# Wide attention with its score channels laid as 128 plus a doubled 64, and transposes issued between the next tile's score matmuls

## The reference, cut to what matters

```python
def _L2_attn_ref(x, Wq, bq, Wk, bk, Wv, bv, Wc, bc):
    B, S, nd = x.shape
    q = jnp.einsum('bsd,ed->bse', x, Wq) + bq
    k = jnp.einsum('bsd,ed->bse', x, Wk) + bk
    v = jnp.einsum('bsd,ed->bse', x, Wv) + bv
    att = jnp.einsum('bqd,bkd->bqk', q, k) * nd ** (-0.5)
    att = jax.nn.softmax(att, axis=-1)
    y = jnp.einsum('bqk,bkd->bqd', att, v)
    y = jnp.transpose(y, (0, 2, 1)).reshape(B, S, nd)
    return jnp.einsum('bsd,ed->bse', y, Wc) + bc
t = t + _L2_attn_ref(_ln_t(t), ...)
```

## Time and profile before

| | us |
|---|---|
| median of 3 executions | 8461.63 |
| lowest, highest | 8458.88, 8468.84 |
| span of the profiled execution | 8460.6 |
| TensorE (PE) busy with matmuls, share of the span | 7417.9, 88% |
| the wide attention's part of the span (first constant issued to last output stored) | about 3369 to 4928 |

### The profile page before, as it was taken

One profiled execution on the slowest core, in us unless ns is written; L12 is line 12 of the kernel. 1 busy time (PEld: TensorE's weight loads), 2 busy tenths in 40 slices (PEclk: granted clock), 3 DMA queues, 4 the chain that ended last, 5 costly groups with the idle time before them and its releaser, 6 DMA issues. The chain is left out here.

```text
span 8460.6 us, 164061 instructions
## 1 busy us (share of the span) xinstructions
PE 7417.9 (88%) x53035; PEld 3625.5 (43%) x53035; DVE 4769.0 (56%) x7714; ACT 3185.4 (38%) x5336; POOL 2338.1 (28%) x2558
## 2 busy tenths in 40 slices
PE   6799999999996775799999970997799999999987
PEld 4233333333333552576666760775433333333326
DVE  6777777777772401232232243114677777777766
ACT  2166666666663241222222210212444444444432
POOL 0011111111111000000000003002388888888861
PEclk8699999999998786899999965998899999999986
DMA  4211111111114314000000031114611111111113
GB/s 118 58 33 33 33 33 33 33 33 33 33 29 95 104 46 132 27 13 13 26 1 17 1 119 54 52 49 135 200 31 30 30 31 29 30 30 31 30 50 105
DMA packets 414311, 426.01 MB, mean 50 GB/s; under 512 B 76199, under 2 KB 386635, under 8 KB 408590
## 3 DMA queue, kind: packets, MB, share of 16 engines
q1 hardware_dynamic: 331790, 339.52, 14.2%
q0 software_dynamic: 62400, 59.16, 2.8%
q10 hardware_dynamic: 19712, 21.53, 0.8%
HBM read 253.37 MB, written 166.55 MB: 50 GB/s over the span
## 5 line engine op out<-in xcount | busy, mean ns | idle before, releaser
L624 DVE TENSOR_REDUCE softmax_part_max<-softmax_ring 128x1 f32<-128x512 f32 (+1 forms) x2880 | 1727.2, 634 | 494.0 <-PE softmax_ring L534 464.0
L2421 DVE TENSOR_TENSOR retention_decayed<-retention_scores,retention_decay_table 128x768 f32<-128x768 f32 x1728 | 1655.4, 958 | 475.0 <-PE retention_scores L2381 475.0
L2440 POOL TENSOR_TENSOR retention_decayed<-retention_third,retention_decay_table 128x384 f32<-128x384 f32 x1728 | 1723.4, 997 | 456.7 <-ACT retention_third L2462 415.5
L664 ACT ACTIVATE softmax_probs<-softmax_scores 128x768 f32<-128x768 f32 x1728 | 1399.2, 811 | 885.8 <-PE softmax_scores L553 847.3
L2462 ACT COPY retention_third<-retention_scores 128x384 f32<-128x384 f32 x1728 | 827.9, 479 | 1276.6 <-PE retention_scores L2381 1276.6
L534 PE MATMUL softmax_ring<-softmax_k_next,softmax_q_next 96*128 96x512 bf16 (+1 forms) x2880 | 1086.5, 379 | 139.7 <-DVE softmax_part_max L624 49.7
L2394 PE MATMUL retention_sums<-retention_decayed,retention_v_piece 128*32 128x288 f32 x13824 | 1197.8, 418 | 0.5 <-POOL retention_decayed L2440 0.5
L2381 PE MATMUL retention_scores<-retention_q_half,retention_k_piece 96*128 96x384 bf16 x5184 | 1145.7, 330 | 29.4 <-DMA retention_v_piece<-ret_v 29.3
L565 PE MATMUL softmax_sums<-softmax_probs,softmax_v_piece 128*32 128x192 f32 x13824 | 930.2, 343 | 0.6 <-ACT softmax_result L653 0.5
L553 PE MATMUL softmax_scores<-softmax_q_third,softmax_k_piece 99*128 99x384 bf16 x3456 | 870.8, 333 | 5.9 <-ACT softmax_probs L664 5.9
L2381 PEld LDWEIGHTS retention_scores<-retention_q_half,retention_k_piece 96*128 96x128 bf16 x5184 | 366.6, 98 | 947.2 <-issue 832.2
(11 more groups left out here) (299 smaller groups left out, 6483.4 us busy)
## 6 DMA issues: line engine op xcount, KB each, us to landing
ret_v<-ret_proj_values SPq DMA_DIRECT2D x8, 1728.0 KB, 8.8
retention_v_piece<-ret_v SPq DMA_DIRECT2D x144, 96.0 KB
softmax_q_third<-rope_q SPq DMA_DIRECT2D x192, 54.0 KB
softmax_q_next<-rope_q POOLq DMA_DIRECT2D x64, 162.0 KB, 3.9
softmax_k_piece<-rope_k SPq DMA_DIRECT2D x192, 54.0 KB
softmax_k_next<-rope_k POOLq DMA_DIRECT2D x64, 162.0 KB, 5.5
ret_q<-ret_proj_parts SPq DMA_DIRECT2D x48, 216.0 KB
ret_k<-ret_proj_parts SPq DMA_DIRECT2D x48, 216.0 KB
```

Source lines behind the costliest of these rows:

```text
L624: nc.vector.reduce_max(part_max[:, j, c:c + 1], ring[m % 2][:, 0:CHUNKS[c][1]], axis=X)\
L664: nc.scalar.activation(probs[n % 4][:, :].rearrange("p (c q) -> p c q", c=2), scores[n % 2][:, :, 0:QC], ACT.Exp, scale=scale).then_inc(ex ...
L2421: nc.vector.tensor_tensor(weights[n % 4][:, 0:2 * QC].rearrange("p (c q) -> p c q", c=2), scores[n % 2][:, 0:2, 0:QC], table[:, table_at(n ...
L2440: nc.gpsimd.tensor_tensor(weights[n % 4][:, 2 * QC:HALF], third[n % 3][:, :], table[:, at:at + QC], ALU.mult)\
```

## The change

- The 192 channels of queries and keys are laid as 128 rows (part 0) plus 64 rows (part 1), and the 64 stand twice, on rows 0 to 63 and on rows 64 to 127. For this `wqk` is loaded in three pieces with the last 64 channels placed twice, the projections write 128 rows instead of 96, and `qk_t` has 128 rows.
- A tile's scores are now five matmuls over 128 channels (`long_part`) and five over 64 (`short_parts`); the short ones take rows 0 to 63 for chunks 0, 2, 4 and rows 64 to 127 for chunks 1 and 3.
- The five long matmuls of the next tile stand between the groups of transposes of this tile (`turn_and_score`); the short ones follow, then `value`.
- `consts_in` counts seven loads instead of five.

```diff
-        wqk, wv = sb("wqk", [HC + 1, 2, 2, 2, HC], F32), sb("wv", [HC + 1, 2, C], F32)
+        wqk, wv = sb("wqk", [HC + 1, 2, 2, 2, P], F32), sb("wv", [HC + 1, 2, C], F32)
...
-        qk_t = sb("qk_t", [HC, 2, 2, N], F32)
+        qk_t = sb("qk_t", [P, 2, 2, N], F32)
...
+        OVER = C - P
...
-            for to, of in [(identity[:, :], ident), (wqk[:, :, :, :, :], w_qk), (wv[:, :, :], w_v),
+            for to, of in [(identity[:, :], ident), (wv[:, :, :], w_v),
                            (wo[:, :, :], w_out), (bo[:, :], out_bias.partition_broadcast(HC))]:
                 sp.dma_start(to, of).then_inc(consts_in, 16)
+            channels = w_qk.rearrange("p h i f c -> p (h i) (f c)")
+            for part, at, of in [(0, 0, channels[:, :, 0:P]), (1, 0, channels[:, :, P:C]), (1, OVER, channels[:, :, P:C])]:
+                sp.dma_start(wqk[:, :, :, part, at:at + (of.shape[2])].rearrange("p h i c -> p (h i) c"), of).then_inc(consts_in, 16)
...
-                        nc.tensor.matmul(bank(n)[0:HC, 0:ln.W], wqk[:, 0, i, half, :], ln.xn[:, 0, chunk], start=True, stop=False)
-                        nc.tensor.matmul(bank(n)[0:HC, 0:ln.W], wqk[0:HC, 1, i, half, :], ln.xn[0:HC, 1, chunk],
+                        nc.tensor.matmul(bank(n)[:, 0:ln.W], wqk[:, 0, i, half, :], ln.xn[:, 0, chunk], start=True, stop=False)
+                        nc.tensor.matmul(bank(n)[:, 0:ln.W], wqk[0:HC, 1, i, half, :], ln.xn[0:HC, 1, chunk],
                                          start=False, stop=True).then_inc(proj_full, 1)
...
-            def score(b, i):
-
-                pe.wait_ge(exped, b * TILES + i)
-                for at, width in CHUNKS:
-                    for f in range(2):
-                        last = nc.tensor.matmul(scores[:, at:at + width], qk_t[:, 0, f, i * P:(i + 1) * P],
-                                                qk_t[:, 1, f, at:at + width], start=(f == 0), stop=(f == 1))
+            def long_part(i, c):
+                at, width = CHUNKS[c]
+                nc.tensor.matmul(scores[:, at:at + width], qk_t[:, 0, 0, i * P:(i + 1) * P], qk_t[:, 1, 0, at:at + width],
+                                 start=True, stop=False)
+
+            def short_parts(i):
+                for c, (at, width) in enumerate(CHUNKS):
+                    rows = slice(c % 2 * OVER, c % 2 * OVER + OVER)
+                    last = nc.tensor.matmul(scores[:, at:at + width], qk_t[rows, 0, 1, i * P:(i + 1) * P],
+                                            qk_t[rows, 1, 1, at:at + width], start=False, stop=True)
                 last.then_inc(scored, 1)
...
+            def turn(b, i, g):
+                t0, n = TGROUPS[g]
+                pe.wait_ge(pt_act, (b * TILES + i) * len(ON_ACT) + (g // 2 if g % 2 == 0 else 0))
+                pe.wait_ge(pt_dve, (b * TILES + i) * len(ON_DVE) + (g // 2 if g % 2 else 0))
...
+            def turn_and_score(b, i):
                 pe.wait_ge(exped, b * TILES + i + 1)
...
+                turn(b, i, 0)
+                for g in range(1, NG):
+                    turn(b, i, g)
+                    if i + 1 < TILES:
+                        long_part(i + 1, g - 1)
+                if i + 1 < TILES:
+                    long_part(i + 1, len(CHUNKS) - 1)
+                    short_parts(i + 1)
...
                 for i in range(TILES):
-                    turn(b, i)
-                    if i + 1 < TILES:
-                        score(b, i + 1)
+                    turn_and_score(b, i)
                     value(b, i)
```

More of the change, by code:

```diff
@@ L1336, in _ @@
             ln.set_ones(pool)
-            pool.wait_ge(consts_in, 80)
+            pool.wait_ge(consts_in, 112)
             with pool.Fori(0, images) as b:
@@ L1364, in projections @@
                         last.then_inc(proj_full, 1)
-            def score(b, i):
-                pe.wait_ge(exped, b * TILES + i)
-                for at, width in CHUNKS:
-                    for f in range(2):
-                        last = nc.tensor.matmul(scores[:, at:at + width], qk_t[:, 0, f, i * P:(i + 1) * P],
-                                                qk_t[:, 1, f, at:at + width], start=(f == 0), stop=(f == 1))
-                last.then_inc(scored, 1)
-            def turn(b, i):
-                pe.wait_ge(exped, b * TILES + i + 1)
[L1377 to L1389, removed]
@@ new lines, in turn @@
+            def turn(b, i, g):
+                t0, n = TGROUPS[g]
+                pe.wait_ge(pt_act, (b * TILES + i) * len(ON_ACT) + (g // 2 if g % 2 == 0 else 0))
+                pe.wait_ge(pt_dve, (b * TILES + i) * len(ON_DVE) + (g // 2 if g % 2 else 0))
+                for k in range(n):
+                    last = nc.tensor.transpose(ring[g % 2][:, k * P:(k + 1) * P],
+                                               probs[i % 2][:, (t0 + k) * P:(t0 + k + 1) * P], identity[:, :])
+                last.then_inc(pt_full, 1)
@@ L1399, in value @@
                 last.then_inc(valued, 1)
-            pe.wait_ge(consts_in, 80)
+            pe.wait_ge(consts_in, 112)
             pe.wait_ge(ln.ones_row, 1)
@@ L1410, in _ @@
                 pe.wait_ge(proj_free, (b + 1) * USES)
-                score(b, 0)
+                for c in range(len(CHUNKS)):
+                    long_part(0, c)
+                short_parts(0)
                 for i in range(TILES):
-                    turn(b, i)
-                    if i + 1 < TILES:
-                        score(b, i + 1)
+                    turn_and_score(b, i)
                     value(b, i)
@@ L1441, in _ @@
                         half, c = divmod(rest, ln.CHUNKS)
-                        nc.scalar.copy(qk_t[:, i, half, c * ln.W:(c + 1) * ln.W], bank(n)[0:HC, 0:ln.W]).then_inc(proj_free, 1)
+                        nc.scalar.copy(qk_t[:, i, half, c * ln.W:(c + 1) * ln.W], bank(n)[:, 0:ln.W]).then_inc(proj_free, 1)
                     else:
```

## The result

| | before | changed |
|---|---|---|
| median | 8461.74 us of 4 | 8316.16 us of 4 |
| lowest to highest | 8458.88 to 8468.84 | 8308.44 to 8325.63 |
| ratio, 95% interval | | 0.9828 [0.9814, 0.9842] |
| span of the profiled execution | 8460.6 | 8324.1 |

The changed kernel is 145.6 us faster; 158.7 were forecast. The profiled execution is the slowest of its four. It is 136.5 us shorter in span than that of before, so I measure the stage by itself, from its first issue on the sync engine to the start of its last row maximum. Before that is 3369.22 to 4886.20, 1517.0 us; after, 3370.16 to 4742.9, 1372.7 us: 144.3 us less.

The account below looks back on a forecast made before the run. TensorE was taken to set the 16.47 us period. Steady periods 153.6 + first periods 6.3 + first scores 5.8 - loads 7 = 158.7 us off the 8460.6 us span: 8301.9, median 8303 us; range 8278 to 8390, chance 0.75.

Parts of the forecast that it names:

- TensorE's sequence sets the period: Steady tile: transposes, scores and values follow on TensorE nearly without a hole, 16.47 us a period, forecast to become 14.07.
- The chain of maximum and exponentials: Scores, maximum, exponentials, next transposes: runs beside the values with 0.65 us to spare and keeps that cover.
- Interleaving removes 0.93 us a tile: Transposes: score matmuls between their groups cover the waits for copies out of the two ring banks, 2.88 to 1.95 us.
- going between transposes and matmuls costs nothing: Steady tile: no cost taken for alternating transposes and full-array matmuls; bad end 0.3 us a tile.
- Short parts 2.15 us, side by side: 64-row score matmuls: two row halves work together, so the longer chain of 5 units decides, 2.15 us against 3.86.
- The serial rival: Short parts: the halves don't run side by side, 3.86 us, 123 us more in all, 8426 us; chance 0.12.
- the rival with bare loads: Short parts: six weight loads of the longer chain aren't hidden, 1.14 us a tile, 82 us, 8385 us; chance 0.07.
- The slow rival: Short parts: each record waits for the one before to leave the array, load bare, 7.4 us, 8681 us; chance 0.02.
- Change of tiling 0.26 us: Going into and out of the row-tiled short parts costs 0.12 + 0.14 us a tile; range 0 to twice that.
- First period of an image, 1.57 us less: First transposes to values, with 4.0 us at half clock: 10.22 us instead of 11.79, four times, 6.3 us.
- First scores, 1.46 us less: First scores of an image, standing alone: 6.27 us instead of 7.73, four times, 5.8 us.
- Loads, 7 us: Stage start: three weight-load issues ahead of `x_in` at 2.48 us each instead of one of 0.28; ends 1 and 28.

Follow-up runs that it names:

- the order alone: Kernel before, with its 96 + 96 layout and loads, but the next tile's score matmul pairs placed between the groups of transposes: 8407.00 us, ratio 0.9936.
- the run on one half: Changed kernel, but all five short parts use rows 0 to 63: 8447.31 us, ratio 0.9985 to the kernel before.
- layout alone: Changed kernel, but all five groups of transposes stand together ahead of the long and short parts: 8375.83 us, ratio 0.9901 to the kernel before.
- the halves in blocks: Changed kernel, but short parts issued in chunk order 1, 3, 0, 2, 4 instead of alternating: 8309.75 us, ratio 0.9817 to the kernel before.

## Why the prediction was right, and where its sizes were off

The result, 8316 us, lies in the range of 8278 to 8390, 13 us above the forecast. Point by point:

- **TensorE's sequence sets the period.** Right. The chain of maximum and exponentials kept its cover.
- **Interleaving removes 0.93 us a tile; going between transposes and matmuls costs nothing.** Right, shown by the order alone: 0.9 us.
- **Short parts 2.15 us, side by side.** Right, and shown by the run on one half: 1.72 us more a tile without it. The serial rival (8426 us) and the rival with bare loads (8385 us) are out. The slow rival is out too: even all ten records on one half take 4.06 us, less than the 4.35 from which it would have decided. (In its price 0.429 + 0.17 is 0.60, not 0.593, which changes nothing. The chances of the serial halves and the slow end, 0.12 and 0.02, are 0.14 together, not 0.16.)
- **Change of tiling 0.26 us.** The mis-sized term that moved the time most: it is 0.39 us in the changed profile, about 0.10 ahead of the first record and 0.10 in it at each of the two changes. A second round trip cost 0.35. The rows that gave the 0.26 run from one tiled step to the next, so they held a whole round trip already; it is cheaper there, with column tiles and bfloat16 matmuls around them, and why is open. With the transposes at 1.97 instead of 1.95 the period is 14.23, not 14.07, and 16 periods of each of four images give 143.1 us instead of 153.6: 10.5 us.
- **First period of an image, 1.57 us less.** It was 10.90 us from the first transposes to the values in the last image, against 11.79 before: 0.89 less. But one image isn't enough here. From the first row maximum of an image to the second, the gain in the four images is 0.9, 0.3, 1.9 and 1.0 us, together 4.1 instead of 6.3. The rows are below.
- **First scores, 1.46 us less.** From the first score to its row maximum 6.51 us against 8.05 (3470.65 to 3478.7): 1.5. Right; with the three stretches between one image's last row maximum and the next one's first (1.8, 1.4 and 1.7 us shorter) it is 6.4 us in all instead of 5.8.
- **Loads, 7 us.** Measured 9.4 us to the first score, between the ends of 1 and 28. The three issues took 20.5 us, where I had 7.4; but the two between them and the first issue fell from 2.48 and 9.48 to 0.28 and 0.67 us. The time shows up at whichever issue comes late in the row, so taking the price from one neighbour's issue came near by luck.

These terms account for the stage: 158.7 - 10.5 - 2.2 + 0.6 - 2.4 = 144.2 us, and it became 144.3 us shorter.

The first period in the four images, from row maximum to row maximum, and for how long after the first transpose the clock still stood at 0.50 (1.2 GHz); behind that it was 1.00 (2.4 GHz):

| image | 1 | 2 | 3 | 4 |
|---|---|---|---|---|
| before: first period, us | 18.53 | 18.52 | 18.63 | 18.74 |
| before: slow clock, us | 2.9 | 3.2 | 3.8 | 4.0 |
| changed: first period, us | 17.59 | 18.23 | 16.78 | 17.74 |
| changed: slow clock, us | 5.0 | 6.1 | 3.3 | 5.3 |

Windows of the changed kernel (busy PE, PEld, DVE, ACT, POOL; PEclk; DMA share; GB/s): a steady stretch, then the second image from its first transpose on, then the third up to the end of the slow clock and behind it. After them the timeline of PE in the last image:

```profile
3655.00:3716.00 61.00, 61.00 (x315) 44.41 (x313) 21.20 (x33) 16.21 (x22) 0.00 (x0) 1.00 0.00 1
3830.95:3837.00 6.05, 6.00 (x16) 3.75 (x17) 0.69 (x1) 1.17 (x2) 0.00 (x0) 0.50 0.00 0
4168.20:4171.50 3.30, 3.25 (x10) 2.33 (x11) 0.69 (x1) 0.59 (x1) 0.00 (x0) 0.50 0.00 0
4171.60:4179.00 7.40, 7.40 (x34) 4.20 (x33) 1.39 (x2) 0.96 (x2) 0.00 (x0) 1.00 0.00 0
```
```profile
4504.23 1.97 PE L1387 MATMUL wide_ring<-wide_identity,wide_probs 128*128 128x128 f32 x8 [6.84 <-ACT wide_probs L1463]
...
4515.13 6.12 PE L1408 MATMUL wide_valued_bank<-wide_v,wide_probs_t 128*128 128x192 f32 x36
```

In the changed kernel every one of the four first periods is 15.1 to 15.2 us and half of its slow stretch, so the clock explains how they differ. The forecast took 4.0 us for the slow stretch from the last image before, which was the longest of its four; in the changed kernel the mean is 4.9. The code is the same in the four images, and the stretch goes from 3.3 to 6.1 us. So this term can't be read from one image, and a forecast of it needs a range. What sets it is not shown. With the transposes in one piece (before and layout alone) it lay between 2.9 and 4.7 us in eight images; with matmuls among them, in the changed kernel and the seven other runs, between 2.8 and 6.2. In the order alone the first period was even longer than before, 19.2 us on average against 18.6. Its slow stretch was longer (3.2 to 6.2 us), and there was hardly a wait to hide: the 18 slow transposes took 4.06 us in one piece before.

## What to carry to other kernels

A sum over 192 rows went faster cut into one full part and a small one that is held twice than in two equal parts: two small matmuls for different output banks then run beside each other on the two halves of the array, and their order of issue made no difference here, even with all four records of one half ahead of the other's. Gather all tiled matmuls of a round in one group, since each change to tiling and back costs 0.35 to 0.39 us here, and put untiled work that doesn't depend on the copies where the transposes would wait. Look at what a new layout does to the loads of its constants: issue the data that the first work needs ahead of them.

## What the runs showed of the hardware that was not expected

- The halves of the array take their matmuls independently of the order of issue: 2.35 us with the halves in blocks, 2.34 alternating.
- A change of tiling costs about 0.10 us ahead of the first records that follow it and 0.10 us in them, on the way in (0.53 us for the first pair instead of 0.43) and on the way out (0.27 us for the first record of the values instead of 0.16).
- Loads in short runs hold the sync engine's queue: three with 1164 runs of 512 and 256 bytes took 20.5 us to issue, one with 97 long rows 0.28 us, though the two issues behind the latter then took 3.54 and 11.98 us.
- After an idle stretch of 6.8 us ahead of an image's first transposes, the time to the full clock differed between images of the same code: 3.3 to 6.1 us in the changed kernel.
